# Gate and last residual of a tile moved from VectorE to GpSimd, with the begin times of the steady batch and of the last one written anew

## The chip, the cores and the metric

The kernel runs on one core of a Trainium2 chip. The metric is the device time of one execution in microseconds (us), the median of three runs. The engines are called as in the profile: PE (TensorE, with PEld for its weight loads), DVE (VectorE), ACT (ScalarE), POOL (GpSimd) and SP (SyncE, which here issues all transfers). SBUF is the on-chip memory that all engines share, PSUM the eight banks that PE writes its sums to.

## What is computed

Eight batches of 1024 rows by 256 columns, in fp32. `mod` gives six rows of 256 numbers for each batch:

```python
sa, ca, ga, sb, cb, gb = (mod[:, 0], mod[:, 1], mod[:, 2], mod[:, 3], mod[:, 4], mod[:, 5])
h = layernorm(x) * (1 + ca) + sa
x = x + ga * attn(h, w_q, w_k, w_v)      # causal, rotary, over all 1024 rows
h = layernorm(x) * (1 + cb) + sb
x = x + gb * ffn(h)                      # the last line: gate and final residual
...
def ffn(x):                              # two layers
    for l in range(2):
        h = shift_token(x)               # half of the columns from the row before
        q, k, v = split(h @ wqkv[l])     # 8 heads of 64, q and k normed, rotary with scale
        x = x + local_attention(q, k, v) @ wo[l]      # window of 128 rows
        h = layernorm(shift_token(x)) * ln_g[l] + ln_b[l]
        a, g = split(h @ w1[l] + b1[l])
        x = x + (a * gelu(g)) @ w2[l] + b2[l]
    return x
```

## The kernel before

**Tiles.** A batch is eight tiles of 128 rows. `X[:, w]` holds tile w of the block's residual stream, `U[:, w]` that of the ffn, both in one SBUF array `xu`. Tile numbers of the ffn run on over batches and layers: tile n = 16 b + 8 l + w, so 56 to 63 are the second layer of batch 3. Products of the big matmuls are made of fp16 high and low halves (three matmuls each).

**Pieces.** The work is cut into pieces, each a short run of instructions on one engine, with a name such as `("yr", n)`. A table `BEGIN` gives a begin time to each piece of one batch; batch b has the same times plus b * `PERIOD`. `ONCE` does it for the loading of weights, and `EDGE` replaces the time of single pieces in single batches (before: 709 pieces, all of the first batch). `schedule()` sorts all pieces by these numbers, and the result is the order in which each engine goes through its pieces. At run time no engine looks at a time: each takes its pieces in that order and waits on semaphores (`at(piece)` is the count to wait for). So the numbers set only orders, and a piece that waits holds up all that stands behind it on its engine. `plan_banks` gives PSUM banks to PE's pieces in the same order. Near the end of a batch the first pieces of the next one (its layer norm, projections, rotary, scores) stand between the last ones of the ffn.

**Names that matter here**, with the lines of the kernel before:

- attention of the next batch: layer-norm statistics (DVE L920, L924; root on POOL L294, L296), normed rows (DVE L936), their transposes on PE (`pp`, L419), scaled on DVE (`af`, L950) and split (`hh` ACT, `hl` POOL L1343); projection (`pj`, PE L431 and L435, copy of v on ACT L702); rotary (`rp` on DVE L970 to L974, sum `ra` on POOL L1348); transposes of q and k (`qt`, PE L445), copied high (ACT L717) and low (DVE L995); scores (`sc`, PE L461); softmax (ACT L730), transposes of its rows (`pt`, PE L472).
- ffn: qkv (`E`, PE L508 and L514), window attention (`G` L547, `H` L565, `I` L581), its normalising on DVE (L1117), output product (`J`, PE L594 and L598), residual (`jr`, DVE L1136), shifted rows by a transfer (`xs`, SP), layer norm (DVE L1145 to L1160), its transposes (`N`, PE L407), first mlp product (`W`, PE L613 and L617), its low half (POOL L1385), second mlp product (`Y`, PE: fifteen matmuls L160 to L162 and two L638).
- end of a tile: `yr` on DVE. L1183 adds the product in PSUM to `U`; for a tile of the second layer L1188 then multiplies `U` by the gate row `modg` and L1190 adds `X`. SP's `os` stores the tile (it waits for `s_fin`, as does `xl`, which loads the next batch's rows into the same `X`), and `mg` loads the next gate row.

Of the kernel before, what the change touches and what calls it, by code (L numbers as in the profile page):

```python
# [46 lines left out]
def adaln_kernel(nc, x, w_q, w_k, w_v, wqkv, q_scale, k_scale, wo, ln_g, ln_b, w1, b1, w2, b2,  # L47
# [3 lines left out]
    with ExitStack() as ctx:  # L51
# [248 lines left out]
        with block:  # L300
# [612 lines left out]
            def _(dve):  # L913
                for piece in ORDER["dve"]:
# [263 lines left out]
                    elif k == "yr":  # L1178
                        n, = ids
                        L, w = divmod(n, NT)  # L1180
                        b = L // DEPTH
                        dve.wait_ge(s_w2, at("Y", n))
                        dve.tensor_tensor(U[:, w, :], ps[:, bank["Y", n], 0:DIM], U[:, w, :], ALU.add).then_inc(s_u2, 1)  # L1183
                        if L % DEPTH == DEPTH - 1:
                            if w == 0:
# [735 lines left out]
```

## Time and profile before

| what | before |
|---|---|
| median of 3 runs | 2638.1 us (2637.03 to 2639.17) |
| span of the profiled execution | 2634.1 us |
| that execution's own time | taken as the median, 4.0 us over its span |
| PE busy | 2526.7 us, 96% |
| DVE busy | 2260.9 us, 86% |
| ACT busy | 1935.6 us, 73% |
| POOL busy | 1303.7 us, 49% |

The profile is of one execution, from its first to its last instruction (the span); what lies between the span and the measured time is start and end outside of it. Busy time is that of instructions at work; an engine that waits on a semaphore is idle. The granted clock of PE is given as a share of full speed (2.4 GHz).

### The profile page before, as it was taken

The numbers are of one execution on the slowest core, as the hardware profiler recorded it, in microseconds if no ns is written. First come the engines' busy times: TensorE is split into PE (matmuls) and PEld (weight loads), VectorE is DVE, ScalarE is ACT, GpSimd is POOL, SyncE is SP. The second block draws the span as 40 slices with busy tenths as digits, with TensorE's granted clock in tenths as the row PEclk, the third lists the DMA queues.
The fourth block names the chain that finished last, engine by engine and source line by source line (L and its number), as shares of the span: only waits on it lengthen the run. The fifth ranks groups of instructions, "written<-read, shape, count | busy, mean of one in ns | idle before, by whom it ended". The sixth has DMA issues, their size and how long they took to land.

```text
span 2634.1 us, 71297 instructions
## 1 busy us (share of the span) xinstructions
PE 2526.7 (96%) x25566; PEld 1725.1 (65%) x25566; DVE 2260.9 (86%) x6247; ACT 1935.6 (73%) x4782; POOL 1303.7 (49%) x953
## 2 busy tenths in 40 slices
PE   7899989999899998999999999999999999999998
PEld 4566666666567665676656666666766666666675
DVE  8997889878898788987889878998889978799785
ACT  3698856888478784788748787587874878658884
POOL 2364535555355554555436554365544555446552
PEclk8999999999999999999999999999999999999999
DMA  5000010000100000000000000000000000000000
GB/s 192 22 7 8 5 43 3 9 5 15 33 3 9 6 17 30 4 10 4 18 29 5 8 5 20 25 6 8 6 19 25 6 8 6 20 25 6 7 6 21
DMA packets 51021, 46.45 MB, mean 18 GB/s; under 512 B 11530, under 2 KB 47980, under 8 KB 50548
## 3 DMA queue, kind: packets, MB, share of 16 engines
q1 hardware_dynamic: 50004, 40.78, 5.0%
q8 instruction: 213, 3.49, 0.6%
q14 instruction: 132, 1.08, 0.1%
q10 hardware_dynamic: 672, 1.10, 0.1%
HBM read 25.06 MB, written 8.42 MB: 13 GB/s over the span
## 4 chain that ended last, share of the span: by engine, by line
PE 69%; DVE 12%; ACT 8%; issue 5%; POOL 4%; DMA 1%; SPq 1%; DVEq 0%; POOLq 0%; ACTq 0%
PE ps L508 10%; PE ps L613 9%; PE ps L581 8%; PE ps L547 6%; PE ps L514 5%; PE ps L617 4%; PE ps L565 4%; PE ps L524 3%; PE ps L594 3%; PE ps L160 2%; PE ps L162 2%; PE ps L161 2%; ACT ar_b L808 2%; PE ps L461 2%; PE ps L407 2%
## 5 line engine op out<-in xcount | busy, mean ns | idle before, releaser
L808 ACT ACTIVATE ar_b<-ar_b,small 128x192 f32<-128x192 f32 (+1 forms) x1024 | 445.2, 437 | 50.4 <-DVE small L1100 48.6
L1366 POOL TENSOR_TENSOR small<-small,neg_half 128x16 f32<-128x16 f32 x128 | 382.2, 2986 | 121.8 <-DVE small L1059 119.9
L1370 POOL TENSOR_TENSOR ar_c<-ar_c 128x1024 f32<-128x1024 f32 x128 | 302.7, 2365 | 282.3 <-DVE ar_c L1086 281.7
L1100 DVE CUSTOM_DVE_ANT_0 ar_b<-ps,mask_t,small 128x192 f32<-128x192 f32 x896 | 319.3, 413 | 29.7 <-PE ps L547 29.2
L1385 POOL TENSOR_TENSOR mlp<-mlp 128x512 f16<-128x512 f32 x160 | 196.3, 1231 | 200.5 <-ACT mlp L863 199.3
L508 PE MATMUL ps<-wqkv_hi,ht_hi 128*128 128x512 f16 x768 | 292.2, 381 | 0.0
L508 PE MATMUL ps<-wqkv_lo,ht_hi 128*128 128x512 f16 x768 | 291.1, 379 | 0.0
L613 PE MATMUL ps<-ht_hi,w_hi 128*128 128x512 f16 (+1 forms) x704 | 268.2, 381 | 5.5 <-ACT ht_hi L759 5.5
L613 PE MATMUL ps<-ht_hi,w_lo 128*128 128x512 f16 (+1 forms) x704 | 267.1, 379 | 0.0
L581 PE MATMUL ps<-ar_b,ar_a 128*64 128x128 f32 x3840 | 239.4, 276 | 0.5 <-DVE ar_b L1124 0.3
L294 POOL TENSOR_SCALAR stats<-stats 128x2 f32<-128x2 f32 x128 | 33.2, 260 | 407.6 <-DVE stats L1149 312.5
L514 PE MATMUL ps<-wqkv_hi,ht_lo 128*128 128x512 f16 x768 | 228.4, 379 | 0.0
L581 PEld LDWEIGHTS ps<-ar_b,ar_a 128*64 128x64 f32 x3840 | 207.2, 137 | 29.7 <-issue 17.4
L617 PE MATMUL ps<-ht_lo,w_hi 128*128 128x512 f16 (+1 forms) x704 | 209.9, 380 | 0.0
L1176 DVE SCALAR_TENSOR_TENSOR mlp<-ps,bias,mlp 128x512 f32<-128x512 f32 x192 | 142.5, 749 | 70.1 <-PE ps L617 33.1
L819 ACT ACTIVATE ar_b<-ar_b,rsw 128x192 f32<-128x192 f32 (+1 forms) x512 | 193.7, 441 | 11.2 <-DVE rsw L1111 10.2
L547 PE MATMUL ps<-ar_a 64*64 64x64 f32 (+2 forms) x5536 | 196.7, 282 | 2.8 <-ACT ar_a L798 2.8
L1124 DVE COPY ar_b<-ps 128x512 f32<-128x512 f32 (+1 forms) x256 | 160.2, 648 | 44.1 <-PE ps L565 44.1
L808 ACT ACTIVATION_READ_ACCUMULATOR ar_b<-ar_b,small 128x1 f32 x1024 | 193.4, 189 | 0.0
L547 PEld LDWEIGHTS ps<-ar_a 64*64 64x64 f32 x5536 | 153.4, 133 | 40.0 <-issue 22.6
L160 PE MATMUL ps<-w_hi,mlp 128*128 128x256 f16 x640 | 175.4, 274 | 0.2 <-POOL mlp L1385 0.2
L162 PE MATMUL ps<-w_hi,mlp 128*128 128x256 f16 x640 | 175.1, 274 | 0.0
(193 smaller groups left out, 6673.3 us busy)
## 6 DMA issues: line engine op xcount, KB each, us to landing
xu<-in_L_attn_x_dram SPq DMA_DIRECT2D x32, 256.0 KB, 2.8
out_dram<-xu SPq DMA_DIRECT2D x64, 128.0 KB, 2.4
rows<-xu SPq DMA_DIRECT2D x128, 63.5 KB
mlp<-in_L_ffn_wqkv_dram SPq DMA_DIRECT2D x2, 1536.0 KB, 6.4
modb<-mod_rows SPq DMA_DIRECT2D x8, 384.0 KB, 4.5
rows<-in_L_ffn_w_dram SPq DMA_DIRECT2D x2, 1364.0 KB, 9.5
rows<-xu SPq DMA_DIRECT2D x112, 0.5 KB
ar_b<-in_L_wmod_dram SPq DMA_DIRECT2D x2, 768.0 KB, 7.4
```

What stands on the lines that cost most here:

```text
L160: pe.matmul(o, a[0], b[0], start=start, stop=False)
L162: return pe.matmul(o, a[1], b[0], start=False, stop=stop)
L508: pe.matmul(ps[:, bk, :], ht[0][:, c, a:a + P], wqkv_p[i][:, L % DEPTH, c, s * INNER:(s + 1) * INNER], start=(c == 0 and i == 0), stop=False)
L514: last = pe.matmul(ps[:, bk, :], ht[1][:, c, a:a + P], wqkv_p[0][:, L % DEPTH, c, s * INNER:(s + 1) * INNER], start=False, stop=(c == 1))
L547: last = pe.matmul(ps[HQ * half:HQ * half + HQ, bk[q], i * KW + o:i * KW + o + m], QT[r:r + HQ, n % 2, hp, HQ * half:HQ * half + HQ], KT[r ...
L581: last = pe.matmul(ps[64 * q:64 * q + 64, bk, (h // 2) * P:(h // 2 + 1) * P], V[:, (n - 1 + kb) % 4, h * DH:(h + 1) * DH], PTW[:, f, q, 2 ...
L613: pe.matmul(ps[0:m, bk, :], q[:, L % DEPTH, c, 2 * j + i, 0:m], ht[0][:, c, a:a + 512], start=(c == 0 and q is w1_p[0]), stop=False)
L617: last = pe.matmul(ps[0:m, bk, :], w1_p[0][:, L % DEPTH, c, 2 * j + i, 0:m], ht[1][:, c, a:a + 512], start=False, stop=(c == 1))
L808: last = act.activation(pw, pw, ACT.Exp, bias=mnw[:, n % 2, h:h + 1], scale=-1.0, accum_out=smw[:, n % 2, h:h + 1])
L1100: dve.tensor_tensor_reduce(out=PW[:, pw_at(f, q, i) + c:pw_at(f, q, i) + KW], in0=ps[:, bk, i * KW + c:(i + 1) * KW], in1=mask, scale=rinv ...
L1366: pool.tensor_tensor(rinv[:, n % 4, :], ssm[:, n % 2, :], neg_half[:, 0:16], ALU.pow).then_inc(s_rinv, 1)
L1370: pool.tensor_tensor(M1[:, n % 2, :], M1[:, n % 2, :], M2, ALU.add).then_inc(s_add, 1)
```

## The change

For each of the 64 tiles of a second layer, the two elementwise instructions behind the residual move from DVE's piece `yr` to a piece `yg` of POOL's. `yr` keeps L1183 (L1182 now) for all tiles. `yg` waits for that add, multiplies by the gate row and adds `X`; stores, loads of the next `X` and of the next gate row wait for `yg` as they did for `yr`.

```diff
@@ DVE @@
                     elif k == "yr":
                         n, = ids
-                        L, w = divmod(n, NT)
-                        b = L // DEPTH
+                        w = n % NT
                         dve.wait_ge(s_w2, at("Y", n))
                         dve.tensor_tensor(U[:, w, :], ps[:, bank["Y", n], 0:DIM], U[:, w, :], ALU.add).then_inc(s_u2, 1)
-                        if L % DEPTH == DEPTH - 1:
-                            if w == 0:
-                                dve.wait_ge(s_modg, 16 * (b + 1))
-                            dve.wait_ge(s_u2, at(*piece))
-                            dve.tensor_tensor(U[:, w, :], U[:, w, :], modg[:, :], ALU.mult).then_inc(s_fa, 1)
-                            dve.wait_ge(s_fa, b * NT + w + 1)
-                            dve.tensor_tensor(U[:, w, :], U[:, w, :], X[:, w, :], ALU.add).then_inc(s_fin, 1)
@@ POOL @@
                         "kk": s_rope, "ul": s_ul, "pz": s_pz}
+                        ... , "yg": s_fin}
+                    elif k == "yg":
+                        n, = ids
+                        L, w = divmod(n, NT)
+                        b = L // DEPTH
+                        pool.wait_ge(s_u2, at("yr", n))
+                        if w == 0:
+                            pool.wait_ge(s_modg, 16 * (b + 1))
+                        pool.tensor_tensor(U[:, w, :], U[:, w, :], modg[:, :], ALU.mult).then_inc(s_fa, 1)
+                        pool.wait_ge(s_fa, b * NT + w + 1)
+                        pool.tensor_tensor(U[:, w, :], U[:, w, :], X[:, w, :], ALU.add).then_inc(s_fin, 1)
@@ tables @@
-PERIOD = 316.98
+PERIOD = 319.81
-    ("D", "pe"): {(0, 0): 37.38, (0, 1): 61.08, ...
+    (new numbers for every piece of BEGIN)
+    (EDGE: 1153 pieces of batch 0, 1155 of batch 1, 1071 of batch 7)
```

The tables are new as a whole: batches 2 to 6 follow `BEGIN`, and batches 0, 1 and 7 have orders of their own by `EDGE`. Three places of the new orders follow, each from the boundary between batches 3 and 4 or from the end of the program.

**PE, end of batch 3, first place.** The last output product of window attention (`J`, L594 and L598), the transposes of the next batch's rows (L419), those of the mlp's rows (L407), the next batch's projection (L431, L435) and the mlp's first product (L613). Before, from the second projection on:

```order
L638 MATMUL ps<-w_lo,rows 128x256
L431 MATMUL ps<-bd_hi,ht_hi 128x384
...
L435 MATMUL ps<-bd_hi,ht_lo 128x384 x2
L407 MATMUL ps<-id_f,rows 128x128 x4
L613 MATMUL ps<-ht_hi,w_hi 128x512
...
L617 MATMUL ps<-ht_lo,w_hi 128x512 x2
L445 MATMUL ps<-id_f,ar_c 128x128 x4
```

After:

```order
L419 MATMUL ps<-id_f,ar_c 128x128 x4
L407 MATMUL ps<-id_f,rows 128x128 x4
L594 MATMUL ps<-wo_hi,rows 128x256
...
L598 MATMUL ps<-wo_hi,rows 128x256 x4
L431 MATMUL ps<-bd_hi,ht_hi 128x384
...
L435 MATMUL ps<-bd_hi,ht_lo 128x384 x2
L445 MATMUL ps<-id_f,ar_c 128x128 x4
L461 MATMUL ps<-ar_a 128x128 x6
L464 MATMUL ps<-mask,id_b 128x128
L407 MATMUL ps<-id_f,rows 128x128 x4
L445 MATMUL ps<-id_f,ar_c 128x128 x4
L613 MATMUL ps<-ht_hi,w_hi 128x512
```

Before, a `Y` (its last row is the first one shown) stood between the transposes and the projections, the second `N` (L407) came next, three blocks of `W` stood ahead of the first transposes of q and k (L445), one more ahead of the second and one ahead of the scores (L461). Now the last `J` stands behind the transposes L419 and the first L407, the projections follow it directly, and L445, the scores L461 and the second L407 stand ahead of `W`.

**PE, a little later, second place.** The last two `Y` of batch 3 (L638 are their last rows), with transposes and scores of batch 4. Before:

```order
L638 MATMUL ps<-w_lo,rows 128x256
L445 MATMUL ps<-id_f,ar_c 128x128 x4
L461 MATMUL ps<-ar_a 128x384 x6
L464 MATMUL ps<-mask,id_b 128x128
L419 MATMUL ps<-id_f,ar_c 128x128 x4
L472 MATMUL ps<-id_f,ar_b 128x128 x3
L445 MATMUL ps<-id_f,ar_c 128x128 x4
L431 MATMUL ps<-bd_hi,ht_hi 128x384
```

After:

```order
L445 MATMUL ps<-id_f,ar_c 128x128 x4
L160 MATMUL ps<-w_hi,mlp 128x256
...
L638 MATMUL ps<-w_lo,rows 128x256
L461 MATMUL ps<-ar_a 128x384 x6
L464 MATMUL ps<-mask,id_b 128x128
L445 MATMUL ps<-id_f,ar_c 128x128 x4
L461 MATMUL ps<-ar_a 128x512 x6
L464 MATMUL ps<-mask,id_b 128x128
L472 MATMUL ps<-id_f,ar_b 128x128 x3
L407 MATMUL ps<-id_f,xu 128x128 x4
L508 MATMUL ps<-wqkv_hi,ht_hi 128x512
```

Before, the scores L461 of four tiles' width stood directly behind their transposes L445, after the last `Y`. Now that `Y` stands between them; the next L445 and its scores follow directly, and behind the softmax's transposes (L472) comes `D` (L407 of `xu`, transposes of the new ffn input), with a block of `E` (L508) directly behind it. In the end of the program `J` of the last tile, 127, was followed by the `Y` of tiles 122 and 123 with an `N` behind each; now by those of tiles 120 to 123, and the rest as before.

**POOL, the first place.** The roots of the layer norms (L294, L296), the low half `hl` that the projection waits for (L1343, now L1335), the rotary's sum `ra` (L1348, now L1340) and the new pieces (L1377, L1379). Before:

```order
L294 TENSOR_SCALAR stats<-stats 128x2
L296 TENSOR_TENSOR stats<-stats,neg_half 128x2
L1343 TENSOR_TENSOR ht_lo<-ar_c,ht_hi 128x2x256
L294 TENSOR_SCALAR stats<-stats 128x2
L296 TENSOR_TENSOR stats<-stats,neg_half 128x2
L1348 TENSOR_TENSOR ar_c<-ar_c 128x512 x2
```

After:

```order
L294 TENSOR_SCALAR stats<-stats 128x2
L296 TENSOR_TENSOR stats<-stats,neg_half 128x2
L1377 TENSOR_TENSOR xu<-xu,modg 128x256
L1379 TENSOR_TENSOR xu<-xu 128x256
L1377 TENSOR_TENSOR xu<-xu,modg 128x256
L1379 TENSOR_TENSOR xu<-xu 128x256
L1335 TENSOR_TENSOR ht_lo<-ar_c,ht_hi 128x2x256
L1340 TENSOR_TENSOR ar_c<-ar_c 128x512
L294 TENSOR_SCALAR stats<-stats 128x2
L296 TENSOR_TENSOR stats<-stats,neg_half 128x2
L1340 TENSOR_TENSOR ar_c<-ar_c 128x512
```

The pieces of tiles 58 and 59 stand now between the root and the low half. Those of 56 and 57 stand ahead of the roots, and those of 60 to 63 in one run at the second place, behind two sums of the rotary. SP's order moved too: stores of batch 3 and loads of batch 4's rows alternate now by pairs of tiles, where three of the four loads stood in a row ahead of all eight stores.

## Rows read from the trace of the kernel before

**Rows 1.** The page: span, busy time of the engines, chain that ended last.

```profile
span 2634.1 us, 71297 instructions
PE 2526.7 (96%) x25566; PEld 1725.1 (65%) x25566; DVE 2260.9 (86%) x6247; ACT 1935.6 (73%) x4782; POOL 1303.7 (49%) x953
PE 69%; DVE 12%; ACT 8%; issue 5%; POOL 4%; DMA 1%; SPq 1%; DVEq 0%; POOLq 0%; ACTq 0%
```

**Rows 2.** Windows: us, busy of PE, PEld, DVE, ACT, POOL; PE's clock, DMA share, GB/s.

```profile
332.10:652.70 320.60, 310.63 (x3195) 212.84 (x3193) 278.21 (x773) 239.51 (x595) 162.82 (x118) 0.99 0.04 13
1013.00:1053.00 40.00, 35.91 (x237) 24.21 (x236) 35.95 (x101) 16.51 (x34) 17.58 (x19) 0.91 0.12 40
1053.00:1073.00 20.00, 20.00 (x149) 14.53 (x148) 19.31 (x43) 11.48 (x20) 6.07 (x9) 1.00 0.00 1
```

**Rows 3.** Timeline of PE, a batch's end: start, us, instruction, [idle before, releaser].

```profile
986.73 0.28 PE L594 MATMUL ps<-wo_hi,rows 128*128 128x256 f16 x1 [0.70 <-ACT rows L837]
...
991.46 0.66 PE L407 MATMUL ps<-id_f,rows 128*128 128x128 f32 x4 [0.37 <-DVE rows L1160]
...
994.29 0.34 PE L431 MATMUL ps<-bd_hi,ht_hi 128*128 128x384 f16 x1 [0.32 <-ACT ht_hi L702]
...
995.45 0.50 PE L435 MATMUL ps<-bd_hi,ht_lo 128*128 128x384 f16 x2 [0.34 <-POOL ht_lo L1343]
...
997.59 0.66 PE L407 MATMUL ps<-id_f,rows 128*128 128x128 f32 x4 [0.66 <-DVE rows L1160]
998.94 0.39 PE L613 MATMUL ps<-ht_hi,w_hi 128*128 128x512 f16 x1 [0.69 <-ACT ht_hi L759]
```

**Rows 4.** Timeline of DVE in the same stretch.

```profile
992.24 0.42 DVE L1190 TENSOR_TENSOR xu<-xu 128x256 f32<-128x256 f32 x1
992.58 0.99 DVE L950 TENSOR_SCALAR ar_c<-ps,modc_all 128x256 f32<-128x256 f32 x2
...
999.52 0.75 DVE L970 TENSOR_TENSOR ar_c<-ps,cos_t 128x256 f32<-128x256 f32 x2
...
1000.58 0.41 DVE L974 TENSOR_TENSOR ar_c<-ps,sin_t 128x256 f32<-128x256 f32 x1
```

**Rows 5.** Timeline of PE, the second place.

```profile
1027.92 0.50 PE L461 MATMUL ps<-ar_a 128*128 128x384 f16 x2 [0.69 <-ACT ar_a L717]
1029.75 1.46 PE L461 MATMUL ps<-ar_a 128*128 128x384 f16 x4 [1.33 <-DVE ar_a L995]
...
1032.87 0.90 PE L472 MATMUL ps<-id_f,ar_b 128*128 128x128 f32 x3 [0.27 <-ACT ar_b L730]
1040.37 0.66 PE L445 MATMUL ps<-id_f,ar_c 128*128 128x128 f32 x4 [1.00 <-POOL ar_c L1348]
```

**Rows 6.** Timeline of ACT there.

```profile
1027.27 0.60 ACT L717 ACTIVATE ar_a<-ps 128x512 f16<-128x512 f32 x1 [5.78 <-PE ps L445]
```

**Rows 7.** Timeline of DVE there.

```profile
1027.75 0.42 DVE L1190 TENSOR_TENSOR xu<-xu 128x256 f32<-128x256 f32 x1
...
1029.04 0.66 DVE L995 TENSOR_TENSOR ar_a<-ps,ar_a 128x512 f16<-128x512 f32 x1
```

**Rows 8.** Groups by line and form: count, busy us, mean ns, idle before.

```profile
L1188 DVE TENSOR_TENSOR xu<-xu,modg 128x256 f32<-128x256 f32 x64 | 27.2, 425 | 2.8
L1370 POOL TENSOR_TENSOR ar_c<-ar_c 128x1024 f32<-128x1024 f32 x128 | 302.7, 2365 | 282.3 <-DVE ar_c L1086 281.7
L1348 POOL TENSOR_TENSOR ar_c<-ar_c 128x512 f32<-128x512 f32 x64 | 81.1, 1268 | 92.8 <-DVE ar_c L974 91.2
```

**Rows 9.** One line's instructions: least, median and greatest ns; when; forms.

```profile
L1117 DVE TENSOR_TENSOR ar_b<-ar_b,rsw x256: 424/558/1419, 121.4 to 2586.5; 128x384 f32<-128x384 f32 x112, 128x256 f32<-128x256 f32 x16
```

**Rows 10.** The chain that ended last, at the program's end.

```profile
2592.83 5.15 DMA rows<-xu
...
2631.03 0.44 DVE xu L1188
```

**Rows 11.** Timeline of PE there.

```profile
2601.12 1.11 PE L407 MATMUL ps<-id_f,rows 128*128 128x128 f32 x4 [4.63 <-DVE rows L1160]
```

More of the change, by code:

```diff
@@ L1317, in _ @@
                 done = {"rt": s_rstd, "hl": s_hl, "ra": s_rot, "r2": s_rstd2, "lt": s_lnr, "pw": s_rinv, "ad": s_add,
-                        "kk": s_rope, "ul": s_ul, "pz": s_pz}
+                        "kk": s_rope, "ul": s_ul, "pz": s_pz, "yg": s_fin}
                 old = None
@@ L1389 @@
 BY_TILE = ("E", "F", "G", "H", "I", "J", "Y", "ev", "sq", "fc", "ex", "na", "hc", "oh", "ss", "x0", "x1", "tm", "nm", "hv", "ol",
-           "jr", "yr", "pw", "ad", "kk", "xs")
+           "jr", "yr", "yg", "pw", "ad", "kk", "xs")
 BY_LAYER = ("D", "N", "Wg", "Wa", "dh", "dl", "nh", "nl", "ls", "lt", "lk", "ge", "us", "uh", "ul")
-PERIOD = 316.98
+PERIOD = 319.81
 BEGIN = {
[203 rows of a table removed]
[203 rows of a table added]
 }
 ONCE = {
-    ("bw", "pe"): {(0, 0): -7.46, (0, 1): 2.64, (0, 2): 8.25, (0, 3): 12.59, (1, 0): 40.81, (1, 1): 45.54,
-        (1, 2): 47.41, (1, 3): 48.84},
-    ("co", "act"): {(0,): -15.41, (1,): 27.89},
-    ("cq", "act"): {(0, 0): 2.68, (0, 1): 6.61, (1, 0): 45.3, (1, 1): 70.45},
-    ("cv", "act"): {(0,): -0.64, (1,): 46.67},
-    ("cw", "act"): {(0, 0): -6.21, (0, 1): 0.82, (1, 0): 31.73, (1, 1): 51.89},
-    ("do", "dve"): {(0,): -13.19, (1,): 29.82},
-    ("dq", "dve"): {(0, 0): 6.25, (0, 1): 8.34, (1, 0): 50.99, (1, 1): 103.49},
-    ("dv", "dve"): {(0,): 1.11, (1,): 85.3},
-    ("dw", "dve"): {(0, 0): 10.54, (0, 1): 21.57, (1, 0): 36, (1, 1): 60.87},
-    ("z0", "dve"): {(): -30.17},
-    ("zM", "pe"): {(): -21.4},
-    ("zR", "pe"): {(): -23.65},
-    ("zT", "pe"): {(): -27.43},
-    ("zW", "pe"): {(): -18.05},
-    ("za", "act"): {(): -30.17},
-    ("zb", "sp"): {(): -5.02},
-    ("zc", "sp"): {(): -29.7},
-    ("zd", "act"): {(): -22.56},
-    ("ze", "act"): {(): -26.54},
-    ("zf", "dve"): {(0,): 19.32, (1,): 53.25},
-    ("zg", "sp"): {(): -21.69},
-    ("zh", "act"): {(): -18.51},
-    ("zi", "dve"): {(): -26.32},
-    ("zk", "dve"): {(): -19.57},
-    ("zl", "dve"): {(): -17.64},
-    ("zm", "sp"): {(): -7.6},
-    ("zn", "dve"): {(): -17.81},
-    ("zo", "sp"): {(0,): -26.98, (1,): -26.5},
-    ("zp", "dve"): {(): -22.56},
-    ("zq", "sp"): {(0,): -7.3, (1,): 10.18},
-    ("zr", "act"): {(): -11.57},
-    ("zs", "sp"): {(): 10.7},
-    ("zt", "dve"): {(): -10.36},
-    ("zu", "dve"): {(): -20.44},
-    ("zv", "sp"): {(0,): -25.48, (1,): 16.46},
-    ("zw", "sp"): {(0,): -26.02, (1,): 23.63},
-    ("zx", "sp"): {(): -6.78},
-    ("zy", "dve"): {(0,): 31.55, (1,): 44.52},
-    ("zz", "dve"): {(): 79.71},
@@ new lines @@
+    ("bw", "pe"): {(0, 0): 24.44, (0, 1): 35.88, (0, 2): 42.36, (0, 3): 46.53, (1, 0): 76.74, (1, 1): 82.64,
+        (1, 2): 85.68, (1, 3): 88.28},
+    ("co", "act"): {(0,): 15.82, (1,): 63.1},
+    ("cq", "act"): {(0, 0): 37.32, (0, 1): 41.26, (1, 0): 82.28, (1, 1): 110.79},
+    ("cv", "act"): {(0,): 33.52, (1,): 83.76},
+    ("cw", "act"): {(0, 0): 28.48, (0, 1): 35.22, (1, 0): 69.39, (1, 1): 92.52},
+    ("do", "dve"): {(0,): 22.38, (1,): 65.6},
+    ("dq", "dve"): {(0, 0): 41.37, (0, 1): 43.29, (1, 0): 88.48, (1, 1): 146.27},
@@ new lines @@
+    ("dv", "dve"): {(0,): 35.71, (1,): 127.38},
+    ("dw", "dve"): {(0, 0): 45.77, (0, 1): 57.23, (1, 0): 71.78, (1, 1): 101.22},
+    ("z0", "dve"): {(): 0},
+    ("zM", "pe"): {(): 12.54},
+    ("zR", "pe"): {(): 11.04},
+    ("zT", "pe"): {(): 6.88},
+    ("zW", "pe"): {(): 16.04},
+    ("za", "act"): {(): 0},
+    ("zb", "sp"): {(): 32.11},
+    ("zc", "sp"): {(): 0.43},
+    ("zd", "act"): {(): 8.96},
+    ("ze", "act"): {(): 8.66},
+    ("zf", "dve"): {(0,): 54.92, (1,): 92.75},
+    ("zg", "sp"): {(): 8.48},
@@ new lines @@
+    ("zh", "act"): {(): 14.97},
+    ("zi", "dve"): {(): 9.07},
+    ("zk", "dve"): {(): 13.76},
+    ("zl", "dve"): {(): 16.67},
+    ("zm", "sp"): {(): 27.03},
+    ("zn", "dve"): {(): 16.32},
+    ("zo", "sp"): {(0,): 3.07, (1,): 3.55},
+    ("zp", "dve"): {(): 10.49},
+    ("zq", "sp"): {(0,): 27.33, (1,): 45.32},
+    ("zr", "act"): {(): 22.32},
+    ("zs", "sp"): {(): 45.97},
+    ("zt", "dve"): {(): 24.42},
+    ("zu", "dve"): {(): 12.16},
+    ("zv", "sp"): {(0,): 4.48, (1,): 52.77},
+    ("zw", "sp"): {(0,): 4.03, (1,): 59.44},
@@ L1643 @@
+    ("zx", "sp"): {(): 27.98},
+    ("zy", "dve"): {(0,): 67.43, (1,): 80.76},
+    ("zz", "dve"): {(): 121.28},
 }
 EDGE = {
[153 rows of a table removed]
[599 rows of a table added]
 }
```

1158 rows, old and new, of tables (BEGIN, EDGE) are left out of this document.

## The prediction

> **What bounds the kernel now.** I read the page first. PE is busy 2526.7 of the span's 2634.1 us and holds 69% of the chain that ended last; DVE has 12% of it, POOL, at 49% busy, 4% [rows 1]. So PE's row of matmuls is the program, and a change gains only where PE stands still. The second view was busy time by windows: one batch takes 320.6 us, of which PE is busy 310.6 [rows 2]. In the middle of a batch PE is busy 20.00 of 20 us, though DVE is busy 19.31 there. But in the 40 us in which one batch ends and the next begins PE works 35.91, at a granted clock of 0.91 of its 2.4 GHz, while DVE works 35.95 [rows 2]. The third view, PE's timeline there, names the waits. In a first place PE waits 0.70 us for ACT before the last `J`, 0.32 and 0.34 before the projection, 0.66 for DVE before an `N`, 0.69 before the first `W` [rows 3]. In a second one, 40 us on, it waits 0.69 and 1.33 at the scores, 0.27 at the softmax's transposes and 1.00 for POOL's rotary sum [rows 5]. The fourth was DVE's timeline beside them, to see what DVE did while PE waited: the copy L950 that the projection needs begins right behind a tile's L1190 [rows 4], and at the second place the low half L995, for which the scores wait until 1029.7, began only at 1029.04, behind another L1190 at 1027.75 [rows 7], although ACT's high half had been ready at 1027.87 [rows 6]. So in both places DVE was late and the two instructions that now leave it stood ahead of what PE waited for.
>
> **The moved instructions.** DVE loses 2 x 64 instructions of 425 ns (L1188's row stands for both lines): 54.4 us in all, 6.8 a batch [rows 8]. POOL gains as many. No row shows POOL's price for 128 x 256 in fp32. Its like are L1348 (512 columns, 1.268 us) and L1370 (1024 columns, 2.365) [rows 8]: 2.14 ns a column and 0.17 us at the start, so 0.72 us at 256. Bounds: 0.43, as on DVE, and 1.27, the row of 512. I take 0.72, the line through the two rows: 1.44 a tile, 92 us in all, and POOL has 1330 us idle [rows 1]. That is no cost by itself; what counts is where a tile's 1.44 us stand in POOL's queue.
>
> They stand in two places. At the first, the pieces of tiles 58 and 59 stand ahead of the low half that the projection waits for. DVE does the residuals of both, then L950 of 0.99, and ACT a high half of some 0.6; POOL may start tile 58's piece about 0.9 us before the residual of 59 is there, so it is done with both some 2.0 us behind that residual, when the low half could have begun after 1.6 to 1.7. POOL is late by about 0.3, and I leave the wait of 0.34 as it is. At the second place four pieces, 5.8 us, stand in one run. Behind them are roots of later rows, whose readers on DVE stand far enough back for them to cost nothing; without that cover it would be up to 5.8 us a batch. A piece waits for its residual, and on SP stores and loads of `X` wait for it; those are not needed for some tiles, so I put nothing on them, and 5.15 us, the transfer nearest by [rows 10], if one came late.
>
> **The first place, by the new order.** A `Y` fills 1.85 us: from the end of the `N` at 991.46 + 0.66 to the wait before the projection, 993.97 [rows 3].
> - The last `J` has the transposes and an `N` ahead of it now, together more than its 0.70: -0.70.
> - The projection's first wait: L950 no longer stands behind two finals: -0.32. The second stays.
> - The second `N` stands behind the scores: -0.66. The `W` behind it has a transposes' group of 0.66 in between: -0.66 of its 0.69.
> - The first transposes of q and k follow the projections without any `W`. Their rotary takes DVE from 999.52 to 1000.99, 1.47 [rows 4], and POOL 1.27 [rows 8], 2.8 with the passing on; only the second projection, 1.1 (eight matmuls from 995.45 to 996.93 [rows 3], six of them), covers it: +1.7.
> - The scores follow these transposes directly and wait for high half (0.60 [rows 6]) and low half (0.66 [rows 7]): +1.3.
>
> Sum: +0.66 us.
>
> **The second place.**
> - Scores: a `Y` (1.85) stands ahead of them, and L995 has 1.7 us less of finals ahead of it on DVE: the 0.69 and 1.33 go, -2.02.
> - Softmax's transposes -0.27, now behind the next tile's scores; the rotary sum's wait goes with the planned distance, -1.00.
> - The next scores follow their transposes directly: +1.3. A block of `E` follows `D` directly and needs its copy on ACT, as long as that of rows 6, with little in between: +0.5.
>
> Sum: -1.49. Both: -0.83 a boundary, seven boundaries: -5.8. The bounds are that none of the new waits shows (-2.34 and -3.29, -5.6 a boundary) and that none of the old ones goes (+3.0 and +1.8, +4.8). Neither end is near, since the old waits are seen and the new ones follow from the order; half of the way to each, some 2.5 us a boundary, goes into the range.
>
> **Tail and start.** After the last tile's `J`, PE waits 4.63 us for the layer norm's rows, at 2601.12 [rows 11]; the chain goes through the transfer of the shifted rows, 5.15 us [rows 10]. Two more `Y` stand behind that `J` now, so it and the transfer come 3.7 earlier, with the same work under them: -3.7, 0 if `J` can't come earlier, for then what is ahead of it waits in the place of the two `Y`. At the very end the two instructions on DVE, 0.44 each [rows 10], become two of 0.72 on POOL, and a semaphore more: +0.7. Batches 0 and 1 have orders of their own; nothing in the view prices them, so 0, with 5 us either way for the range.
>
> **Sum.** -5.8 - 3.7 + 0.7 = -8.8: span 2625.3. The profiled execution's time lies 4.0 us over its span, as the median does, so 2629.3, say 2629. Beneath 0.2%, 5.3 us, the measurement tells no change: from 2632.8 to 2643.4 it is the same.
>
> **A page that speaks against the change.** L1117, on DVE with two inputs from SBUF, takes 0.424 us at least, 0.558 in the median and 1.419 at most [rows 9], though its shapes differ by half only. The Trainium skill, GPSIMD Engine Reference, section 8 (Key points), says that GpSimd shares its SBUF interfaces with VectorE and that the two contend when a VectorE instruction reads two inputs from SBUF, and that VectorE is about twice as fast at elementwise work. The row agrees in that the longest is three times the shortest. By the factor of two an instruction would take 0.85 us on POOL, an estimate; the end would cost 0.9 instead of 0.7, and the sum come to 2629.5 instead of 2629.3. What the sharing could do to the time is rival 3, worked out from rows.
>
> **Rivals.**
> 1. *More is won.* With PE's waits shorter the granted clock may stay at 1.00 in the 40 us that now show 0.91 [rows 2]: 3.4 us a boundary, 24 in all, 2629 - 24 = 2605. For it: it is 1.00 in the window right behind, where PE is busy throughout. Against: five new waits stand in the same stretch.
> 2. *Nothing to tell.* The new waits are as long as the old ones, and the table, made anew as a whole, puts others into the middle of the batch, 0.8 us of them in 300. Then only the tail is left: 2638.1 - 3.0 = 2635.
> 3. *Slower, by POOL's work on SBUF.* Eight pieces of 1.44 us, 11.5 in all, lie in the stretch of a batch where DVE is busy 36 of 40 us [rows 2]. If DVE stands still for half of these 11.5 us, as L1117's spread allows [rows 9], 5.8 of the 6.8 that it was spared are gone: the old waits stay and the new ones come on top, +4.8 a boundary at the worst against my -0.83. Half of the way there is 2.8 more a boundary: 2629.3 + 7 x 2.8 = 2649. It decides for slower from 2.0 us a boundary (2629.3 + 14.1 = 2643.4); from 0.5 on it takes the gain below what can be told. For it: the row's spread, and that the stretch is DVE's fullest; against: most of DVE's work there reads PSUM, and POOL has only 17.6 us of work in it.
>
> **Chances and range.** Forecast (2615 to 2632.8): 0.42. Rival 1 (below 2615): 0.13. Rival 2 (2632.8 to 2643.4): 0.23. Rival 3 (above): 0.22. Faster is the forecast and rival 1, 0.55; same 0.23; slower 0.22. A tenth on either side may fall out: down to 2609, into rival 1, and up to rival 3's 2649. The forecast's own range is 2615 to 2633.
>
> **What would show it.** Right: L1377 and L1379 of 0.7 us on POOL; a batch of 319.8; PE without a wait at the four-wide scores, but with 1.7 before the first L445 behind the projections; in the tail a wait of about 1 us before the last `N`, with the transfer 3.7 earlier. Wrong: a wait for POOL's low half or for its roots, then POOL's queue is the bound; L1117 and other two-input lines of DVE longer beside L1377, then it is SBUF; a granted clock of 1.00 over the boundary; or PE waits in the middle of a batch, where it is busy throughout now.

## The result, and the profile after

The changed kernel takes 2829.6 us, median of four runs (2827.8 to 2836.1), the kernel before 2637.6: a ratio of 1.0731, 95% interval 1.0716 to 1.0746. It is 192 us slower, far outside the predicted range. The page of the profile after, span and busy time:

```profile
span 2834.3 us, 71277 instructions
PE 2610.6 (92%) x25566; PEld 1730.1 (61%) x25566; DVE 2286.5 (81%) x6119; ACT 1943.6 (69%) x4768; POOL 1414.5 (50%) x1081
```

PE executes the same 25566 matmuls in 84 us more of busy time and stands still for 116 us more than in [rows 1]. DVE, from which 128 instructions were taken, is busier by 26 us. So there are waits, a lower clock on PE, and instructions of DVE that became longer.

Busy time by windows, with the columns of [rows 2]: one batch; two stretches of its middle; its end.

```profile
1099.40:1446.60 347.20, 320.64 (x3189) 211.78 (x3188) 281.25 (x756) 240.90 (x592) 176.33 (x134) 0.98 0.04 12
1164.50:1186.20 21.70, 20.44 (x221) 12.90 (x222) 21.46 (x55) 17.21 (x53) 9.76 (x5) 1.00 0.08 23
1273.00:1294.70 21.70, 19.40 (x177) 10.28 (x176) 16.14 (x52) 16.06 (x45) 7.61 (x6) 0.92 0.02 5
1403.20:1424.90 21.70, 13.26 (x65) 6.94 (x64) 12.56 (x37) 6.19 (x11) 6.84 (x9) 0.76 0.10 29
```

A batch takes 347.2 us instead of 320.6 [rows 2]. PE's idle time in it rose from 10.0 to 26.6 us, its busy time from 310.6 to 320.6. The worst window is the end of the batch, 13.26 of 21.70 us at a clock of 0.76, but the middle, where PE had worked 20.00 of 20 us, is open as well: 1.3 and 2.3 us of idle in 21.7.

PE's waits over the whole program (who waits, for whom, then us in total, times, longest), and one of DVE's:

```profile
PE ps L407 <- DVE rows L1160: 44.2, 18, 9.5
PE ps L461 <- DVE ar_a L995: 25.6, 7, 5.6
PE ps L565 <- DVE ar_b L1117: 19.3, 21, 1.9
PE ps L160 <- DVE ar_b L1002: 14.2, 15, 2.4
PE ps L445 <- POOL ar_c L1340: 13.7, 9, 1.9
PE ps L638 <- POOL rows L1387: 12.6, 8, 2.0
```
```profile
DVE stats L1145 <- DMA rows<-xu: 50.2, 24, 5.0
```

L407 behind L1160 is the `N` that waits for the rows of the ffn's layer norm. L461 behind L995 are the scores that wait for their low half: one of the seven waits stands at the program's start (0.6 us), the others at six boundaries, 5.3 to 5.6 us at four of them, 2.0 and 1.4 at two. At the first and at the last boundary the longest wait is that of L407, 6.7 and 9.5 us. L1145 is DVE's own wait for the shifted rows; about half of its 50.2 us lies at the seven boundaries. The timeline of PE at one first place, the counterpart of [rows 3]:

```profile
1402.91 0.61 PE L598 MATMUL ps<-wo_hi,rows 128*128 128x256 f16 x4 [0.38 <-DVE rows L1130]
...
1404.53 0.50 PE L435 MATMUL ps<-bd_hi,ht_lo 128*128 128x384 f16 x2 [0.36 <-POOL ht_lo L1335]
...
1407.94 0.66 PE L445 MATMUL ps<-id_f,ar_c 128*128 128x128 f32 x4 [1.94 <-POOL ar_c L1340]
1409.28 0.40 PE L461 MATMUL ps<-ar_a 128*128 128x128 f16 x2 [0.69 <-ACT ar_a L717]
1415.13 0.61 PE L461 MATMUL ps<-ar_a 128*128 128x128 f16 x4 [5.46 <-DVE ar_a L995]
```

SP's queue and DVE's timeline under that last wait:

```profile
1403.45 0.40 SPq L310 DMA_DIRECT2D xu<-in_L_attn_x_dram  x1
1404.01 0.63 SPq L335 DMA_DIRECT2D rows<-xu  x1
```
```profile
1406.46 0.47 DVE L1142 BATCH_NORM_STATS2 stats<-xu 128x6 f32<-128x128 f32 x2
1410.36 0.49 DVE L1145 BATCH_NORM_STATS2 stats<-rows 128x6 f32<-128x128 f32 x2 [3.42 <-DMA rows<-xu]
...
1412.68 1.29 DVE L1160 TENSOR_SCALAR rows<-rows,stats 128x128 f32<-128x128 f32 x1
...
1414.40 0.68 DVE L995 TENSOR_TENSOR ar_a<-ps,ar_a 128x512 f16<-128x512 f32 x1
```

After the last `J` (1402.91) the residual and the transfer of the shifted rows must run before the ffn's statistics. The transfer, issued at 1404.01, is there for DVE at 1410.36, 6.35 us later. DVE stands in L1145 for 3.42 us of that; the rotary of the next tile, the normed rows and L995, for which the scores wait, stand behind it in DVE's queue. One of the normed rows, L1160, took 1.29 us beside GpSimd's rotary sum L1340 (1412.59 to 1413.88), where its median is 0.34. Before, PE had 12.2 us from the begin of the last `J` (986.73) to the first `W` (998.94) [rows 3] over this chain, with two `Y`, transposes, an `N` and the projections in them. Now all four `Y` of tiles 56 to 59 stand ahead of the `J`.

At the second place and at the end, PE's timeline (in the first row nothing is waited for):

```profile
1447.01 1.14 PE L461 MATMUL ps<-ar_a 128*128 128x384 f16 x6
...
1449.34 0.60 PE L461 MATMUL ps<-ar_a 128*128 128x512 f16 x2 [0.69 <-ACT ar_a L717]
...
1452.99 0.39 PE L508 MATMUL ps<-wqkv_hi,ht_hi 128*128 128x512 f16 x1 [0.69 <-ACT ht_hi L751]
...
2802.84 0.66 PE L407 MATMUL ps<-id_f,rows 128*128 128x128 f32 x4 [2.29 <-DVE rows L1160]
```

Groups of GpSimd by line, and all instructions of L1059 on DVE (least, median and greatest ns):

```profile
L1377 POOL TENSOR_TENSOR xu<-xu,modg 128x256 f32<-128x256 f32 x64 | 48.0, 749 | 59.2 <-DVE xu L1182 42.0 <-issue 17.1
L1379 POOL TENSOR_TENSOR xu<-xu 128x256 f32<-128x256 f32 x64 | 46.9, 733 | 5.0
```
```profile
L1059 DVE TENSOR_SCALAR small<-small x128: 174/175/2641, 114.9 to 2762.0; 128x16 f32<-128x16 f32 x128
```

The finals cost what was forecast, 0.749 and 0.733 us. That an instruction of 175 ns can take 2641 is taken up below.

### The profile page after: what moved, and what is told of

The parts are those of the page before. It is cut to its first block and busy times, and to the rows that moved or that the text cites. A ratio compares the mean times of both kernels' runs of the same rounds, so it can differ in the third digit from the quotient of the medians.

```text
span 2834.3 us, 71277 instructions
## 1 busy us (share of the span) xinstructions
PE 2610.6 (92%) x25566; PEld 1730.1 (61%) x25566; DVE 2286.5 (81%) x6119; ACT 1943.6 (69%) x4768; POOL 1414.5 (50%) x1081
## 5 line engine op out<-in xcount | busy, mean ns | idle before, releaser
L1358 POOL TENSOR_TENSOR small<-small,neg_half 128x16 f32<-128x16 f32 x128 | 403.4, 3153 | 238.0 <-DVE small L1059 234.4
L1362 POOL TENSOR_TENSOR ar_c<-ar_c 128x1024 f32<-128x1024 f32 x128 | 303.2, 2369 | 404.3 <-DVE ar_c L1086 403.2
L508 PE MATMUL ps<-wqkv_hi,ht_hi 128*128 128x512 f16 x768 | 297.8, 388 | 7.3 <-ACT ht_hi L751 7.3
L1387 POOL TENSOR_TENSOR mlp<-mlp 128x512 f16<-128x512 f32 x160 | 186.1, 1167 | 224.4 <-ACT mlp L863 224.0
L508 PE MATMUL ps<-wqkv_lo,ht_hi 128*128 128x512 f16 x768 | 296.0, 385 | 0.0
L613 PE MATMUL ps<-ht_hi,w_hi 128*128 128x512 f16 (+1 forms) x704 | 273.1, 388 | 3.9 <-ACT ht_hi L759 2.1
L613 PE MATMUL ps<-ht_hi,w_lo 128*128 128x512 f16 (+1 forms) x704 | 271.7, 386 | 0.0
L581 PE MATMUL ps<-ar_b,ar_a 128*64 128x128 f32 x3840 | 252.2, 278 | 2.0 <-ACT ar_b L827 1.2
L581 PEld LDWEIGHTS ps<-ar_b,ar_a 128*64 128x64 f32 x3840 | 205.9, 136 | 43.9 <-issue 34.2
L547 PE MATMUL ps<-ar_a 64*64 64x64 f32 (+2 forms) x5536 | 211.4, 290 | 8.4 <-ACT ar_a L798 7.8
L565 PEld LDWEIGHTS ps<-id_f,ar_b 64*128 64x128 f32 x3840 | 139.4, 139 | 92.7 <-issue 52.7
L294 POOL TENSOR_SCALAR stats<-stats 128x2 f32<-128x2 f32 x128 | 36.9, 288 | 311.6 <-DVE stats L1149 190.2
L565 PE MATMUL ps<-id_f,ar_b 64*128 64x64 f32 x3840 | 170.7, 229 | 22.8 <-DVE ar_b L1117 19.3
L827 ACT ACTIVATE ar_b<-ps 128x512 f32<-128x512 f32 (+1 forms) x256 | 143.3, 566 | 68.6 <-PE ps L565 65.3
## 6 DMA issues: line engine op xcount, KB each, us to landing
rows<-xu SPq DMA_DIRECT2D x128, 63.5 KB
```

Of the source, the lines that this page charges most:

```text
L508: pe.matmul(ps[:, bk, :], ht[0][:, c, a:a + P], wqkv_p[i][:, L % DEPTH, c, s * INNER:(s + 1) * INNER], start=(c == 0 and i == 0), stop=False)
L547: last = pe.matmul(ps[HQ * half:HQ * half + HQ, bk[q], i * KW + o:i * KW + o + m], QT[r:r + HQ, n % 2, hp, HQ * half:HQ * half + HQ], KT[r ...
L565: last = pe.transpose(ps[:, bk[half], o:o + HQ], PW[r:r + HQ, c:c + P], id_f[r:r + HQ, r:r + HQ])
L581: last = pe.matmul(ps[64 * q:64 * q + 64, bk, (h // 2) * P:(h // 2 + 1) * P], V[:, (n - 1 + kb) % 4, h * DH:(h + 1) * DH], PTW[:, f, q, 2 ...
L613: pe.matmul(ps[0:m, bk, :], q[:, L % DEPTH, c, 2 * j + i, 0:m], ht[0][:, c, a:a + 512], start=(c == 0 and q is w1_p[0]), stop=False)
L1358: pool.tensor_tensor(rinv[:, n % 4, :], ssm[:, n % 2, :], neg_half[:, 0:16], ALU.pow).then_inc(s_rinv, 1)
```

## The experiments

Two theories stood at the start: the tables' new order makes the loss, or the finals on GpSimd do. Ratios are to the kernel before, with the 95% interval, always.

**One half of the change at a time.** The first kernel keeps the old order and moves only the finals; the second keeps the new order and puts the finals back into DVE's `yr`.

```diff
 # old order, finals on GpSimd: code of yr and yg as in the change, tables as before
+    made += [(round(time + 0.55, 2), "pool", ("yg", q[1])) for time, _, q in made
+             if q[0] == "yr" and q[1] // NT % DEPTH == DEPTH - 1]
 # new order, finals on DVE: code of yr as before, tables as in the change
+    made = [m for m in made if m[2][0] != "yg"]
```

> The order of before on every engine, with the two instructions of a tile's end on GpSimd, each pair put into its queue right behind the point where the residual on VectorE is planned. Theory A (the new order costs the time, not GpSimd): 2630 to 2645 us, within 0.3% of before, since VectorE is spared 6.8 us a batch and GpSimd has room. Rival B (GpSimd's finals cost it, by SBUF or by its queue): most of the 192 us is here, 2780 us or more; a tenth of it or more a batch already at the boundary.

> The order of after on every engine, but gate and final residual stay on VectorE, right behind the tile's residual as before. Theory A (order): 2815 to 2850 us, as slow as after or a little slower. Rival B (GpSimd's finals): 2640 to 2680 us, near before.

Measured: 0.9959 (0.9946 to 0.9973), 2628.7 us, and 1.0764 (1.0743 to 1.0784), 2842.5 us. Moving the finals gains 0.4% in the old order and 0.3 points in the new one, where the two intervals overlap a little. The order alone loses 7.6%. The first of the two is faster than both given kernels.

**Where in the batch.** Each piece was given the changed kernel's time in one part of every batch and the old time elsewhere (finals on GpSimd): 100 us around each of the seven boundaries, or the middle of batches 1 to 6.

```diff
 # the rule of the tables in short, not code of the kernel
-BEGIN/ONCE/EDGE of the change
+cuts = [t for b in range(7) for t in (295 + b * 316.98, 395 + b * 316.98)]
+# between the cuts of a boundary the new times, elsewhere the old; for the other kernel the reverse
```

> Finals on GpSimd. The order of after in the seven stretches of 100 us around the batch boundaries (from the last tiles of one batch's window attention to the first qkv blocks of the next ffn), the order of before elsewhere. Theory A1 (half of the loss lies at the boundaries: about 6 us of waits and 4 us of half clock a batch): 2690 to 2720 us. Rival A2 (nearly all of it there): 2780 or more. Rival A3 (nearly none): 2640 or less.

> Finals on GpSimd. The reverse: the order of after in the middle of batches 1 to 6, the order of before around the boundaries and in the first and last batch. A1: 2680 to 2715 us (about 9 us of waits and 2 of half clock in each of six). A2: 2640 or less. A3: 2780 or more.

Measured: 1.0389 (1.0373 to 1.0404) and 1.0419 (1.0402 to 1.0437). Beside 0.9959 that is 4.3% for the boundaries and 4.6% for the middles, where the whole new order costs 7.7%: each hybrid has seams of its own, so the shares are rough, but neither part is small, and both lie above the 2720 and 2715 us that were expected at most if each had half. Waits of PE in the first, then in the second:

```profile
PE ps L461 <- DVE ar_a L995: 26.2, 7, 5.6
PE ps L407 <- DVE rows L1160: 20.8, 3, 9.5
```
```profile
PE ps L407 <- DVE rows L1160: 37.6, 27, 4.6
PE ps L565 <- DVE ar_b L1117: 21.8, 26, 1.4
PE ps L547 <- ACT ar_a L798: 17.1, 20, 1.0
```

The scores' wait of 5.5 us is the boundary's, complete. The middle has others: many short ones in the window attention, and of its 27 waits for the layer norm twelve are those of the first layer in batches 1 to 6 (1.7 and 2.3 us, 23.9 in all). Fourteen more, of 0.4 to 1.0, stand at the boundaries as in the old order, and one is the tail's. The wait of 2.3 is made by the same chain as the one at the boundary, as the changed kernel shows on DVE and PE:

```profile
932.72 0.49 DVE L1145 BATCH_NORM_STATS2 stats<-rows 128x6 f32<-128x128 f32 x2 [2.29 <-DMA rows<-xu]
936.11 0.66 PE L407 MATMUL ps<-id_f,rows 128*128 128x128 f32 x4 [2.28 <-DVE rows L1160]
```

Busy time in the old order with the finals on GpSimd (span 2627.6 us), with the new order at the boundaries (2737.1) and in the middle (2748.3):

```profile
PE 2524.5 (96%) x25566; PEld 1724.0 (66%) x25566; DVE 2215.1 (84%) x6119; ACT 1935.7 (74%) x4782; POOL 1396.3 (53%) x1081
PE 2556.7 (93%) x25566; PEld 1730.1 (63%) x25566; DVE 2241.7 (82%) x6119; ACT 1943.5 (71%) x4782; POOL 1395.1 (51%) x1081
PE 2568.2 (93%) x25566; PEld 1718.6 (63%) x25566; DVE 2246.0 (82%) x6119; ACT 1940.2 (71%) x4770; POOL 1419.9 (52%) x1081
```

PE stands still for 103, 180 and 180 us. The waits of the scores make 20 of the 77 us that the boundaries add, so most of what the boundary costs is spread over other waits. The mean granted clock is 0.987, 0.970 and 0.985: a lower clock comes with the boundaries, and hardly with the middle, though PE is busy there for 44 us more.

**The wait for the shifted rows.** Statistics and normed rows read `U` instead of the transferred rows, so that DVE doesn't wait there; the token shift is left out, the transfer still runs.

```diff
-dve.wait_ge(s_xs[l * 4 + p], ...)
-last = dve.bn_stats(stw[:, w, 1, :], XS[:, w, :])
+last = dve.bn_stats(stw[:, w, 1, :], U[:, w, P:DIM])   # the normed rows likewise; yr now waits for s_xs
```

> After, but the mlp's layer norm takes the second half of the columns from the row itself and not from the row before, so it doesn't wait for the transfer of the shifted rows; the transfers are still made, and the tile's residual waits for them later. The token shift of the mlp is left out of the result. Theory T (the transfer's 5 to 6 us are what the new order leaves uncovered, at the boundary and in the middle): 9 us of waits a batch and their clock go, 2700 to 2760. Rival U (the waits are those of chains over PE, ACT and DVE, and the transfer only shows first): 2800 or more, since the next link is late too.

> The same edit on before, as the control: the token shift of the mlp is left out. Both theories: 2620 to 2633 us, since before waits for the transfer 8.8 us in all on VectorE, 4.6 of them in the tail.

Measured: 1.0540 (1.0525 to 1.0556), 2781.1 us, and 0.9984 (0.9975 to 0.9994), 2635.3 us, for the same edit in the kernel before. It gives back 1.9 points, 50 us, where before it gave 4 us. That lies between the two theories' ranges, and the control misses its own by 2 us. The waits named above shrink:

```profile
PE ps L407 <- DVE rows L1159: 14.7, 10, 4.3
PE ps L461 <- DVE ar_a L995: 10.5, 7, 2.1
```

So this wait, at the boundaries and in the middle together, is the largest single part found, but a quarter of the loss.

**Can the boundary be mended by order alone?** One kernel puts the `Y` of two tiles back behind the last `J` at all seven boundaries; one puts DVE's statistics behind the low half L995 of the next scores (six of seven).

```diff
 # T is the table of begin times; the rule in short, not code of the kernel
+T["Y", n + 10] = T["J", n + 15] + 0.3;  T["Y", n + 11] = T["pj", b + 1, 1] + 0.3   # their yr, yg, os, xl behind
+# the other kernel: ls, lt, lk, N of the last pair
+T["ls", L, 3] = T["ql", b + 1, 0] + 0.01;  T["lt", L, 3], T["lk", L, 3], T["N", L, 3] behind it
```

> After, with two second products (tiles 58 and 59, and their like at all seven boundaries) behind the last output product and not ahead of it, as before had them; residuals, finals, stores and the next load of these two tiles follow them. Theory T (what the boundary lost is the cover of the transfer): the wait of 5.2 us at the first scores falls by 3.7 or more, with some half clock, 35 to 55 us in all: 2775 to 2795. Rival W (the output product comes no earlier, for its own chain loses the two as cover): 2815 or more.

> After, with the statistics and rows of the last tile pair's layer norm (L1142 to L1160, its root on GpSimd, its transposes on PE) behind the low half of the next batch's first scores, at six of seven boundaries. If VectorE's order is the matter: the wait at the scores falls below 1.5 us and no other takes its place, 3 us or more a boundary with the clock, 2790 to 2812. If the transfer's latency is: the wait comes back at the last N, 2818 to 2832.

Measured: 1.0772 (1.0756 to 1.0788) and 1.0708 (1.0690 to 1.0726). The first is worse: what stood ahead of the `J` had used those `Y` as cover in its turn, and L581 waits 16.9 us in nine places, while L995's wait shrinks only from 25.6 to 20.3. In this kernel SP issues the shifted rows ahead of the store and the load that stand in front of them in the changed kernel. SP's queue and DVE there:

```profile
1402.73 0.60 SPq L335 DMA_DIRECT2D rows<-xu  x1
```
```profile
1407.91 0.49 DVE L1145 BATCH_NORM_STATS2 stats<-rows 128x6 f32<-128x128 f32 x2 [0.59 <-DMA rows<-xu]
```

The transfer takes 5.18 us here, and as long in the old order with the finals on GpSimd (986.83 to 992.01). In the changed kernel, 0.56 us behind a load of 256 KB, it took 6.35. So some 1.2 us of the scores' wait come with SP's new order and not with PE's; no run moves SP's order alone.

In the second the wait of 5.46 is 0.44, and PE then waits for the `N` of the same chain. PE's timeline there:

```profile
1399.82 0.61 PE L461 MATMUL ps<-ar_a 128*128 128x128 f16 x4 [0.44 <-DVE ar_a L995]
...
1403.31 1.12 PE L407 MATMUL ps<-id_f,rows 128*128 128x128 f32 x4 [1.92 <-DVE rows L1160]
```

Over the program L995's wait falls from 25.6 to 4.4 us and L407's rises from 44.2 to 49.7, but the time falls by 0.2 points only, and the intervals overlap: DVE's order at this place is worth nothing that can be told. That the chain of `J`, transfer and statistics needs independent work of PE under it is how I read the two kernels; neither shows the boundary mended.

**The tail alone.** Old order with the finals on GpSimd, and the `Y` of tiles 120 and 121 behind the last `J`.

```diff
 # T as above
+T["Y", 120] = T["J", 127] + 0.5;  T["Y", 121] = T["J", 127] + 0.6   # their yr, yg and os follow
```

> The first experiment's kernel (old order, finals on GpSimd) with one thing of the new order: in the last batch the second products of tiles 120 and 121 stand behind the last output product, so that four and not two lie under the transfer of the shifted rows. The prediction's tail term: 3.7 us less than that kernel's 2628.7, so 2624 to 2627. Rival: nothing (2628 to 2630), since what stood ahead of the output product waits in their place.

Measured: 0.9963 (0.9949 to 0.9977), the 0.9959 of the same kernel without it. PE's timeline shows where the gain went:

```profile
2570.14 0.88 PE L547 MATMUL ps<-ar_a 64*64 64x192 f32 x16 [1.78 <-ACT ar_a L798]
```

A wait of 1.78 for ACT before a `G`, and one of 1.74 before an `H`, stand now where the two `Y` stood.

**GpSimd and VectorE on SBUF.** L1117 takes 2739 ns at most now (1419 in [rows 9]), and the time that DVE's instructions take above the median of their own line and shape, summed over the program where it is 60 ns or more, rose from 33.8 to 104.9 us. One case, on GpSimd, DVE and PE:

```profile
1174.87 2.35 POOL L1362 TENSOR_TENSOR ar_c<-ar_c 128x1024 f32<-128x1024 f32 x1 [5.51 <-DVE ar_c L1086]
1174.91 2.72 DVE L1117 TENSOR_TENSOR ar_b<-ar_b,rsw 128x384 f32<-128x384 f32 x1
1177.69 0.71 PE L565 MATMUL ps<-id_f,ar_b 64*128 64x64 f32 x16 [1.24 <-DVE ar_b L1117]
```

L1117 starts 0.04 us behind a GpSimd add of 1024 columns and ends 0.4 us behind its end, which is about its own least time: it stood still for the add's whole length. The kernel with the new order and the finals on DVE has 103.8 us of such excess, the old order with the finals on GpSimd 41.9: it comes with the order, which puts rotary adds beside window attention, and not with the moved finals. Four edits test what it costs; each also takes work out of a chain that PE waits for, so none prices the hold alone. One halves the sums of squares on DVE; one drops the clip L1059, so that the root reads the sums; one cuts the add L1362 to 128 of its 1024 columns; the last takes all reliefs, the shifted rows' too, and halves ACT's squares as well. Each has its control in the old order with the finals on GpSimd (0.9959 unedited).

```diff
+SQ.rearrange("p (h d) -> p h d", d=DH)[:, :, 0:DH // 2]                 # half the sums
-dve.tensor_scalar(ssm[:, n % 2, :], ss[:, n % 2, :], 1e-24, None, ALU.max)   # no clip; pow reads ss
+pool.tensor_tensor(M1[:, n % 2, 0:P], M1[:, n % 2, 0:P], M2[:, 0:P], ALU.add)   # short add
```

> After, with the sum of squares of q and k taken over half of each head's columns: 0.6 us less on VectorE for each of 128 tiles, 9.7 us a batch, all in the ffn; the result leaves out the other half of the squares. Theory V (in the middle the new order puts VectorE's work so close that PE waits for it): 4 us a batch or more come back, 2750 to 2795. Rival X (single links are too short, VectorE's sum doesn't matter): 2815 to 2830.

> The same edit on the first experiment's kernel (old order, finals on GpSimd), as the control, with the same part left out: V and X both 2615 to 2629, for PE hardly waits in the middle there.

> After without VectorE's small clip of the sums of squares (L1059, 128 x 16, never active for these inputs): GpSimd takes the root of the sums themselves. In after these 128 instructions take 0.174 us alone and up to 2.64 beside a GpSimd instruction, 35 us over their median in all. Theory Z (VectorE's two-port instructions, held while GpSimd works on SBUF, make the new order's chains late): 40 us or more come back, 2760 to 2790. Rival (the held time is slack elsewhere): 2805 to 2825.

> The same edit on the old order with finals on GpSimd, where the clip is held for 9 us only. Both theories: 2622 to 2629, up to 6 us better than without the edit.

> After, with GpSimd's rotary sum of the ffn (L1362, 128 x 1024, 2.37 us, 128 of them) done on 128 of its 1024 columns; the other columns leave the second term out. It takes 2 us off every chain through it and 16 x 2 us a batch off GpSimd and SBUF. Theory Z2 (GpSimd's hold on SBUF and its chains are the rest of the loss): 60 us or more come back, 2700 to 2770. Rival: 2790 to 2825.

> The same edit on the old order with finals on GpSimd, the control: 2620 to 2629, since PE waits little there.

> After with all edits at once: no wait for the shifted rows, no clip, squares and their sums over half of each head, the short add; left out are what these leave out. If latencies and holds of the other engines are the whole loss: within 40 us of the control, 2600 to 2660. If they only add up: 2700 to 2740. If PE's order itself costs it: 2740 or more.

> All the same edits on the old order with finals on GpSimd, the control: 2595 to 2622.

Measured, new order and then control:

| edit | new order | old order |
|---|---|---|
| none | 1.0731 (1.0716 to 1.0746) | 0.9959 (0.9946 to 0.9973) |
| half the sums | 1.0664 (1.0649 to 1.0679) | 0.9945 (0.9931 to 0.9958) |
| no clip | 1.0619 (1.0605 to 1.0632) | 0.9955 (0.9943 to 0.9967) |
| short add | 1.0594 (1.0578 to 1.0610) | 0.9981 (0.9971 to 0.9991) |
| all | 1.0375 (1.0360 to 1.0391) | 0.9931 (0.9916 to 0.9946) |

The clip, 175 ns alone and 22 us in all by its median, is worth 1.1 points in the new order and nothing that can be told in the old; the short add is worth 1.4 points there and nothing here. The first three miss the gains that were expected if DVE's work or the hold were the main cause (2795, 2790 and 2770 us at most; measured 2815.5, 2802.2 and 2794.0). So the new order is sensitive to work that the old one hides. All together give back 3.6 points, less than the 5.1 of their sum, and 4.4 points (117 us) remain between the two orders. PE's largest waits then:

```profile
PE ps L407 <- DVE rows L1158: 14.7, 10, 4.3
PE ps L445 <- POOL ar_c L1340: 12.9, 8, 2.0
PE ps L638 <- POOL rows L1387: 12.6, 8, 2.0
PE ps L565 <- DVE ar_b L1116: 11.0, 13, 1.4
```

No single one is left to blame. What remains is spread over waits for DVE, ACT and GpSimd, most of them of 2 us or less. Between the two profiled executions (2734.8 and 2621.6 us) PE stands still for 53 us more and is busy for 60 us more (2584.4 and 2524.6); by the mean clocks of 0.979 and 0.986 some 21 of the 60 are the clock's, an estimate. The rest was not split further and stays open.

## Why the prediction was wrong, step by step

**POOL's price: right.** 0.72 forecast, 0.749 and 0.733 measured; that is 1.7 to 1.8 times DVE's 0.425, not the two of the estimate beside it. **Low half behind the finals: right**, 0.36 where 0.34 was kept. In the old order the move gives 0.4%, so that half of the change was understood. The 4.0 us between span and time were not: the profiled execution after has 1.8 (2834.3 and 2836.1), and so have the other runs. That shifts the forecast by 2 us and decides nothing.

**The first place, +0.66: wrong, and the first step that failed.** Its term for q and k's transposes was right (1.7 forecast, 1.94). The term of the scores was 1.3 and measured 0.69 + 5.46. The old waits of 0.66 and 0.69 behind the last `J` were struck out because the `N` stands later in PE's order now; but its rows still come through residual, transfer and statistics, and DVE's statistics stand ahead of the scores' low half. The transfer's 5.15 and the wait of 4.63 were in [rows 10, 11] and were used for the tail alone. The kernel without the shifted rows' wait prices the chain at 50 us, the middle's share of it included; with DVE's statistics moved PE waits for the `N` of the same chain. The step was one of several: for -5.8 us at the boundaries the kernel with the new order there shows 4.3 points, 113 us, and a large part of its new waits, such as 1.65 us before a `Y` for its low half on GpSimd (L638, at six boundaries 1.65 to 1.95), stood in no term.

**The second place, -1.49: as forecast at the rows that it names.** The scores behind the last `Y` wait for nothing at 1447.01. (They are of 128x384, three tiles wide, not four as said ahead of the prediction.) The next ones, 128x512, wait 0.69 for ACT and not for the low half (1.3 forecast); `E` behind `D` waits 0.69 (0.5 forecast).

**The middle, put at nothing: wrong, and about as dear as the boundaries.** The prediction looked at the order at the boundaries and took 20.00 of 20 us busy for a property of the middle. It was a property of the old order: the new times in the middle alone cost 4.6 points, some 121 us, against the old order with the same finals. That pieces with a long chain behind them lost the independent matmuls that covered it is how I read it; shown is that the order there makes the waits, 2.3 us of them in each batch by the shifted rows' chain.

**Tail, -3.7: the place was right, the sum wrong.** PE waits 2.29 before the last `N` instead of 4.63, but the tail moved alone gains nothing: the two `Y` had covered a `G` and an `H` ahead of the `J`. The prediction named that case as its bound of 0. **End, +0.7: right**; from the end of the last `Y` to the end of the program 4.3 us instead of 3.6.

**The rivals.** The first, a clock back at 1.00, went the other way: 0.967 over the span instead of 0.987. The second had waits in the middle, but 0.8 us of them a batch, where the new middle costs some 20. The third, slower by GpSimd's work on SBUF, has the right side with the wrong cause: the finals on DVE are slower still. Its mechanism exists, in other instructions: the rotary adds against DVE's attention work.

## What to carry to other kernels

Where engines run in a fixed order, a matmul that waits for nothing is cover for some chain; before moving it earlier, list every chain that it covered, from the producer through residual, transfer and statistics back to PE, and price each with its own rows. A table made anew is a change of the whole period: compare the order in the middle as closely as in the places that the change speaks of, and take a fully busy stretch as the old order's merit. To judge such a change, run its halves apart first; here that found the part worth keeping (finals on GpSimd, 0.9959) at once.

## What the runs showed of the hardware

A GpSimd add can hold a VectorE instruction for its whole length: L1117 took 2.72 us beside an add of 2.35. L1059, 175 ns in the median, took 2641 ns in this stretch of GpSimd and DVE:

```profile
448.01 2.36 POOL L1362 TENSOR_TENSOR ar_c<-ar_c 128x1024 f32<-128x1024 f32 x1
448.32 2.64 DVE L1059 TENSOR_SCALAR small<-small 128x16 f32<-128x16 f32 x1
450.32 1.27 DVE L1002 TENSOR_TENSOR ar_b<-ps,ar_b 128x512 f16<-128x512 f32 x2
450.78 0.15 POOL L1346 MEMSET ar_b<- 128x64 f32 x1
```

DVE's next instruction begins at 450.32, where the add ends (450.37); the record of L1059 runs on until GpSimd's memset behind it is done. So DVE was held for 2.0 us there, and the sums of excess above are upper bounds. The Trainium skill, SBUF — State Buffer, section "SBUF: two separate sides", says that the port pair which the two engines share is an exclusive lock, that a VectorE instruction takes part in it in a mode that uses both ports, or with two SBUF inputs against a GpSimd instruction that reads SBUF, and that the loser is blocked for the other's whole instruction. The rows of L1117 agree. What was unexpected is that order alone, with the same instructions, moved the sum of excess from 41.9 to 104.9 us.

A transfer of 63.5 KB within SBUF took 5.18 us from issue to reader in two kernels, and 6.35 where SP issued it 0.56 us behind a load of 256 KB.

PE's clock was 0.76 in the window with 8.4 us of idle in 21.7, 0.92 with 2.3 and 1.00 with 1.3, but also 1.00 with 3.7 (1142.80 to 1164.50): the sum of idle time alone doesn't tell it. Over a batch, busy time rose by 10.0 us for the same work beside 16.6 us more of waits, so that each microsecond of waiting that the profile shows came with 1.6 of time. The clock is only a part of that, since the new order in the middle has 44 us more of busy time at nearly the same clock. Another part the profile can't show: PE's rows of 128x512 last 0.38 us and follow each other after 0.22 (1452.99 and on), so a wait below 0.16 us between two of them counts as busy time. How much that is was not measured.
